# Attention stacks and the high halves of q and k: transposed by DMA instead of by TensorE and ScalarE, with SyncE in an order of steps of its own

## The reference, cut to what matters

```
x = x + cross_attention_16_heads(layernorm(x), ctx)       # stage n (projections) and stage a (attention)
x = x + quantised_ffn_with_conv(layernorm(x))              # stage b
x = x + cross_attention_1_head(layernorm(x), ctx)          # stage d
x = x + mixture_of_8_experts(layernorm(x))                 # stage c
```

```
q = rms_norm(x @ Wq + bq)                 # 16 heads of width 8
k, v = rms_norm(ctx @ Wk + bk), ctx @ Wv + bv
attn = softmax(q @ k.T / sqrt(8))         # per head, 128 x 120
out = (attn @ v) @ Wproj + bproj
```

## Time and profile before

| | us |
|---|---|
| median of 3 runs | 1326.22 (1324.22 to 1331.3) |
| the profiled execution, its own time | 1328.85 |
| its span, from the first to the last instruction | 1327.0 |
| TensorE busy | 1172.4 (88%) |
| VectorE busy | 1068.7 (81%) |
| ScalarE busy | 872.2 (66%) |
| GpSimd busy | 691.5 (52%) |
| chain of work that ended last | TensorE 60%, VectorE 29%, ScalarE 5% |

### The profile page before, as it was taken

How to read it: one execution, slowest core, us unless ns; L and a number is a source line. 1 busy time by engine, 2 the same in 40 slices (tenths; PEclk the granted TensorE clock), 3 DMA queues, 4 the chain that set the end, 5 groups by cost and what they waited for, 6 DMA issues and landing times.

```text
span 1327.0 us, 27899 instructions
## 1 busy us (share of the span) xinstructions
PE 1172.4 (88%) x10338; PEld 825.1 (62%) x10338; DVE 1068.7 (81%) x2837; ACT 872.2 (66%) x1684; POOL 691.5 (52%) x827
## 2 busy tenths in 40 slices
PE   1567578999999999999999999999999999989998
PEld 1334345776757676766767676767677576756665
DVE  4567786889899888889898998898888897767553
ACT  0245365868767676867777676768686676856554
POOL 3211214566564828374565738284756537365665
PEclk9567778999999999999999999999999899999999
DMA  6000001001010101010010101010100101000000
GB/s 190 20 13 9 20 16 28 17 15 38 3 42 9 43 9 36 16 37 16 5 41 10 43 9 43 9 36 17 35 17 6 31 1 36 16 9 16 9 8 9
DMA packets 63846, 32.69 MB, mean 25 GB/s; under 512 B 29280, under 2 KB 63072, under 8 KB 63328
## 3 DMA queue, kind: packets, MB, share of 16 engines
q1 hardware_dynamic: 61696, 26.83, 8.1%
q10 hardware_dynamic: 2016, 4.08, 0.8%
HBM read 24.73 MB, written 4.19 MB: 22 GB/s over the span
## 4 chain that ended last, share of the span: by engine, by line
PE 60%; DVE 29%; ACT 5%; issue 3%; POOL 1%; DMA 0%; SPq 0%; POOLq 0%; DVEq 0%; ACTq 0%
PE py L699 12%; PE pa L531 5%; DVE q_st L1075 4%; PE pg L682 3%; PE pa L495 3%; DVE moe L1196 3%; PE pa L519 3%; PE pu L682 3%; PE pg L684 3%; PE pg L683 3%; PE pu L683 3%; PE pu L684 3%; DVE acc L1209 2%; PE pb L579 2%; DVE stats L973 2%
## 5 line engine op out<-in xcount | busy, mean ns | idle before, releaser
L897 POOL TENSOR_TENSOR moe<-moe 128x512 f32<-128x512 f32 x256 | 325.0, 1272 | 410.0 <-DVE moe L1196 291.4
L699 PE MATMUL py<-wd_s,moe 128*128 128x128 f32 x2048 | 272.4, 277 | 1.7 <-ACT side L830 1.7
L699 PEld LDWEIGHTS py<-wd_s,moe 128*128 128x128 f32 x2048 | 258.0, 192 | 23.4 <-issue 3.8
L820 ACT ACTIVATE tg<-pg 128x512 f32<-128x512 f32 x256 | 153.2, 598 | 107.6 <-PE pg L684 106.0
L1075 DVE TENSOR_REDUCE q_st<-pa 128x4 f16<-128x480 f32 x256 | 167.7, 655 | 58.4 <-PE pa L495 58.3
L1196 DVE SCALAR_TENSOR_TENSOR moe<-tg,pg 128x512 f32<-128x512 f32 x256 | 174.0, 680 | 45.3 <-ACT tg L820 45.0
L834 ACT ACTIVATE moe<-pu 128x512 f32<-128x512 f32 x256 | 153.9, 601 | 33.4 <-PE pu L684 30.6
L758 ACT ACTIVATE probs<-pa 120x512 f32<-120x512 f32 x256 | 139.3, 602 | 16.7 <-PE pa L519 15.9
L495 PE MATMUL pa<-kbd,qkht 128*128 128x480 f16 x256 | 101.5, 397 | 38.6 <-DVE q_st L1075 33.4
L682 PE MATMUL pg<-x4h,wg_h 128*128 128x512 f16 x256 | 99.1, 387 | 14.9 <-DVE moe L1196 13.1
L682 PE MATMUL pu<-x4h,wu_h 128*128 128x512 f16 x256 | 99.0, 387 | 0.0
(11 more groups left out here) (182 smaller groups left out, 2529.0 us busy)
## 6 DMA issues: line engine op xcount, KB each, us to landing
xin<-in_x SPq DMA_DIRECT2D x16, 256.0 KB, 2.8
xres<-in_x SPq DMA_DIRECT2D x16, 256.0 KB, 3.0
kbd<-qkht SPq DMA_DIRECT2D x256, 7.5 KB
out_x<-acc SPq DMA_DIRECT2D x16, 256.0 KB, 4.1
ctxt_a<-in_ctx_t SPq DMA_DIRECT2D x16, 240.0 KB, 2.6
ctxt_b<-in_ctx_t SPq DMA_DIRECT2D x16, 240.0 KB, 3.5
ctxn_b<-in_ctx SPq DMA_DIRECT2D x16, 240.0 KB, 4.2
wd_s<-in_wd ACTq DMA_DIRECT2D x1, 1024.0 KB, 8.6
```

Of the source, the lines that this page charges most:

```text
L699: mm = pe.matmul(py[:, j, :], hu[:, u % 3, j * S:(j + 1) * S], wd_s[:, u, :], start=(half == 0 and j == 0), stop=(half == 1), skip_group_c ...
L820: act.activation(tg[:, u % 2, :], pg[:, :], ACT.Tanh, scale=0.5 / WSCALE).then_inc(tg_done.sem, 1)
L897: pool.tensor_tensor(hu[:, u % 3, :], gw[:, u % 3, :], us[:, u % 3, :], ALU.mult)\
```

## The change

What it does:

- Step `qkht` and step `stacks` no longer exist on TensorE and ScalarE. SyncE issues DMA transposes from SBUF to SBUF instead. For each group: one of `k_hi` (4 blocks of 128 x 128, fp16), one of `q_hi` (4 blocks), one of all k stacks of the group (16 blocks), and, for each t, one of the q stack (4 blocks). That is 7 DMAs and 40 blocks (1.31 MB) in each period.
- The q stack of t is double-buffered in `qs_t2`, the k stacks of a group in `ks_t2`. `k_st` is now single-buffered, and `kbd` is filled from `kht`.
- SyncE gets strings of its own in `TURNS`, and those of all other engines are written anew.
- `xq` and `p1n` are removed; their steps work in place in `xn2` and `p1`. Two waits come with that.

In the full period the steps of SyncE that do something stand in this order: `stacks` 0, `stacks` 1, load of xin, `stacks` 2, loads of ctxt_b and ctxn_b, load of ctxt_a, `stacks` 3, transpose of `k_hi` (in `rms_k`), transposes of `q_hi` and of the k stacks (in `rms_q`), the 16 DMAs into `kbd` (in `qkht`), store of the output, load of xres. On TensorE the new order between `max` (0, 3) and `scores` (0, 0) holds `g` 2, `u` 2, `d` 0, `g` 3 and `u` 3 of stage c; in `abdc` it holds `g` 2, `u` 2 and `d` 0. On VectorE the steps `fused` (one addition over 128 x 512) and `ln4` (a layernorm's statistics) now follow the making of `q_hi`; before they preceded it.

```
     "pe": {
...
-        "nabdc": ("bcadcacbaccacnacaccaaabaacadbcabccdbaaccabbaccbaacbabnadabcdbabccbacnaccabccnaacabacbccaadcabccd"
-                  "bacdacbacdnccccnabanacccdcbcacdbacca"),
...
+        "nabdc": ("accaacbcacccaccbanacaabcaaccbddccbcabdabcnbcanabcaabcbcancbaacanbdcbabcaaccacbccaaccdbaaccbadnad"
+                  "abccbaccdbcanccbaaccaccbaadcbadcacad"),
...
+    "sp": {
...
+        "nabdc": ("aacccccccbbbacacbabbcccacaacacaaaccacbnadccbaccdccbaacandabbccabcdcccccaaaadbaabdabdbbcacdbnccn"
+                  "dcbcadccabcaacaabbaaacnnbacccnacdaba"),
...
-        st_t = sb("st_t", [128, NQ * (S + SC)], F16)
+        qs_t2 = sb("qs_t2", [128, 2, NQ, S], F16)
+        ks_t2 = sb("ks_t2", [128, 2, GB, NQ, 128], F16)
...
+            def do_n(step, g):
+                if step == "xn1t" and g < NG - 1:
+                    sp.wait_ge(xn1_done.sem, xn1_done.at(g))
+                    sp.dma_start(xin[:, :, :], x_g[g + 1]).then_inc(xin_in.sem, 16)
+                elif step == "qkv" and g < NG - 1:
+                    sp.wait_ge(v_ps.sem, v_ps.at(g))
+                    sp.dma_start(ctxt_a[:, :, :], ctxt_g[g + 1]).then_inc(ctxa_in.sem, 16)
+                elif step == "rms_k":
+                    sp.wait_ge(kh_done.sem, kh_done.at(g))
+                    if later(g):
+                        for part in kbd_in:
+                            sp.wait_ge(part.sem, part.at(g - 1, 16 * HQ))
+                    sp.dma_start_transpose(kht[:, :, :], heads(k_hi)).then_inc(kht_in.sem, 16)
+                elif step == "rms_q":
+                    sp.wait_ge(q_hi_done.sem, q_hi_done.at(g))
+                    sp.dma_start_transpose(qht2[:, g % 2, :, :], heads(q_hi)).then_inc(qht_in.sem, 16)
+                    sp.wait_ge(dup_done.sem, dup_done.at(g, 2))
+                    sp.wait_ge(kl_done.sem, kl_done.at(g))
+                    if g >= 2:
+                        sp.wait_ge(s_ps.sem, s_ps.at(g - 2, 2 * GB))
+                    sp.dma_start_transpose(ks_t2[:, g % 2, :, :, :].rearrange("p t n s -> p (t n) s"),
+                                           k_st[:, :, :, :].rearrange("p t h d -> p (t h d)")).then_inc(ks_in.sem, 16)
+                elif step == "qkht":
+                    sp.wait_ge(kht_in.sem, kht_in.at(g, 16))
+                    if later(g):
+                        sp.wait_ge(max_ps.sem, max_ps.at(g - 1, 4 * GB))
...
+                        sp.dma_start(kbd[rows, :, h, :], kht[rows, :, 0:SC]).then_inc(kbd_in[h // HQ].sem, 16)
+
+            def do_a(step, g):
+                name, t, c = named(step)
+                if name == "stacks":
+                    if t == 0:
+                        sp.wait_ge(dup_done.sem, dup_done.at(g, 2))
+                        sp.wait_ge(ql_done.sem, ql_done.at(g))
+                    sp.wait_ge(max_done.sem, max_done.at(g, 4 * t + 4))
+                    if t >= 2:
+                        sp.wait_ge(s_ps.sem, s_ps.at(g, 2 * t - 2))
+                    elif later(g):
+                        sp.wait_ge(s_ps.sem, s_ps.at(g - 1, 2 * (GB + t) - 2))
+                    sp.dma_start_transpose(qs_t2[:, t % 2, :, :],
+                                           q_st2[:, g % 2, t, :, :].rearrange("p h d -> p (h d)")).then_inc(qs_in.sem, 16)
...
-                elif name == "stacks":
...
-                    take(BM, st_done, g, t + 1)
-                    for n in range(NQ):
-                        pe.transpose(pm16[:, n * S:(n + 1) * S], q_st[:, t, HQ * n:HQ * n + HQ, :], id_h[:, :])
-                    for n in range(NQ):
-                        mm = pe.transpose(pm16[:, NQ * S + n * SC:NQ * S + (n + 1) * SC],
-                                          k_st[0:SC, t, HQ * n:HQ * n + HQ, :], id_h[0:SC, 0:SC])
...
                     if c == 0:
-                        pe.wait_ge(st_done.sem, st_done.at(g, t + 1))
+                        if t == 0:
+                            pe.wait_ge(ks_in.sem, ks_in.at(g, 16))
+                        pe.wait_ge(qs_in.sem, qs_in.at(g, 16 * (t + 1)))
...
-                    act.activation(st_t[:, :], pm16[:, 0:NQ * (S + SC)], ACT.Copy).then_inc(st_done.sem, 1)
```

More of the change, by code:

```diff
@@ L80 @@
         "n": "nnnnnnn",
[L81 to L89, removed]
+        "wna": "nnaanaaaaaanaaanaawaaaaaaaaawaaawanaawwaaaaaaaaaaaaaan",
+        "nab": "aaabaaabababaaaanbbabaaaababbaanababaaaabbaaaanbabbaaababnnabaababbabnaan",
+        "nabd": "bbbbadaaabdnabbabbabaabadbanadabbaaaaanaabdaabaabdaabnaaaababnaaaddabanbaaadbnadbada",
+        "nabdc": ("abcaccacbcacccaacadacbaccacnbdcbccbbadancbbbcaaacacacbabaabccabdcccnacbcccaaabdcacaabdcabcbcnaca"
+                  "dcnbdaacnncaabccacbaccbcaacdadaccdab"),
+        "abdc": ("cabccacbacdcabaacccbaaccabadcabbcdabacdacccaabacbacaacacccabbcabaacccabcacbccdacaaccdccbadbccaba"
+                 "aabacaadcdbccacbdcbccabdcacba"),
+        "bdc": "cbccbcccdcbcbbbccbdcbcdbbcccbbcbcccdcbccccccddbccbccbcccdccbbddcccbcccbcdcccbccbdbc",
+        "dc": "cccccccccccccccddccccdccccdcdcccccccdccddccdccccccccccccddc",
         "c": "cccccccccccccccccccccccccccccccccccccccccccccccc",
@@ L106 @@
         "n": "nnnnnnn",
[L107 to L113, removed]
@@ new lines, in do_d, with do_c @@
+            def do_d(step, g):
+                if step == "oc" and g < NG - 1:
+                    sp.wait_ge(oc_ps.sem, oc_ps.at(g))
+                    sp.dma_start(ctxt_b[:, :, :], ctxt_g[g + 1]).then_inc(ctxb_in.sem, 16)
+                    sp.dma_start(ctxn_b[0:SC, :, :], ctx_g[g + 1]).then_inc(ctxb_in.sem, 16)
+            def do_c(part, g):
+                if part == ("d", NU - 1):
+                    sp.wait_ge(sum_done.sem, sum_done.at(g, len(SIDE)))
+                    sp.dma_start(out_g[g], acc2[:, :, :]).then_inc(out_done.sem, 16)
@@ L426, in _, with idle @@
+            def idle(step, g):
+                pass
+            periods(sp, lambda n, a, b, d, c: run_turns("sp", n, a, b, d, c, idle, do_n, do_a, idle, do_d, do_c))
             sp.wait_ge(out_done.sem, out_done.at(NG - 1, 16))
@@ L473, in do_n @@
                     mm.then_inc(v_ps.sem, 1)
-                elif step == "qkht":
-                    qkh = bank("qkht").bitcast(F16)
-                    pe.wait_ge(q_hi_done.sem, q_hi_done.at(g))
-                    take(BANK["qkht"], qkht_done, g)
-                    for j in range(GB):
-                        pe.transpose(qkh[:, j * S:(j + 1) * S], q_hi[:, j, :], id_h[:, :])
-                    pe.wait_ge(kh_done.sem, kh_done.at(g))
-                    for j in range(GB):
-                        mm = pe.transpose(qkh[:, GB * S + j * SC:GB * S + (j + 1) * SC], k_hi[0:SC, j, :],
-                                          id_h[0:SC, 0:SC])
-                    mm.then_inc(qkht_ps.sem, 1)
             def do_a(step, g):
                 name, t, c = named(step)
-                q_st, k_st, v_st = q_st2[:, g % 2, :, :, :], k_st2[:, g % 2, :, :, :], v_st2[:, g % 2, :, :, :]
+                v_st, ks_t, qs_t = v_st2[:, g % 2, :, :, :], ks_t2[:, g % 2, t, :, :], qs_t2[:, t % 2, :, :]
                 if name == "max":
@@ L634, in do_d @@
                     for j in range(GB):
-                        mm = pe.transpose(pd[0:SC, j * S:(j + 1) * S], p1n[:, j, :], id_f[:, :])
+                        mm = pe.transpose(pd[0:SC, j * S:(j + 1) * S], p1[:, j, :], id_f[:, :])
                     mm.then_inc(p1t_ps.sem, 1)
```

162 lines of the change are left out of this document (74 added, 88 removed).

## The result

The changed kernel takes 1351.12 us (median of 4 runs, 1349.64 to 1353.46); the kernel before, measured beside it, 1327.83. The ratio is 1.0177, with a 95% interval of 1.0144 to 1.0211. The forecast was 1315, on the other side of no change; 1351 lies in its range. The span of the profiled execution is 1349.5 us against 1327.0, 22.5 us more.

A forecast was written before the change was run, and what follows sets the result against it. It took TensorE to bound full periods, VectorE close behind. Removed work -31.8, stalls +11.7 and early periods +8.9 summed to -11.2 us, hence 1315 us; range 1298 to 1395, likeliest case 1301 to 1326.

The forecast's parts named there:

- The step that failed: Full periods: TensorE busy 69 of 72 us, VectorE 65 and 7 behind, so work taken off TensorE counts.
- Rival 2: VectorE sets the full period, so relief and stall vanish and +8.9 us of early periods remain: 1335 us; chance 0.12.
- Removed work: TensorE's transposes and its wait for the first stack's copy: 2.51 us per full period, 31.8 us in all.
- The price of a transpose: SyncE's time issuing a DMA transpose: 1.04 us for a q stack, 2.1 us for the k stacks.
- The stall at the first stack: TensorE before scores (0, 0): latency 3.2 us, 2.4 covered, 0.8 open; 2.1 in abdc; together 11.7 us.
- SyncE's queue and kbd: Full periods: kbd's last quarter arrives 1.2 us before it is needed; k stacks may cost SyncE 3.3 us.
- Rival 1: SyncE's queue late with kbd behind the k stacks: 1369 to 1465 us; chance 0.20 at moderate prices, 0.12 near upper bound.
- Early periods: wna, nab, nabd: q stack latency 7.2 us, plus 1.7 for the first kbd being late; 8.9 us added.
- The clock (rival 3): New stall lowers the granted clock in every second full period, adding 39 us: 1354 us; chance 0.06.

The follow-up runs named there:

- the long memsets: GpSimd's 256 multiplies gw * us replaced by three memsets each, product left out: changed kernel 1301.98 us, kernel before 1321.90 us.
- the halves: Each GpSimd multiply gw * us done as two of 256 columns, nothing left out: changed kernel 1320.82 us, kernel before 1343.86 us.
- the run with each twice: Changed kernel with a second DMA transpose of 4 blocks, into a spare tile, behind each of the seven from the third group on: 1363.47 us.
- the old order: Changed kernel with TensorE, ScalarE, VectorE and GpSimd in the kernel before's order of steps, SyncE keeping its new one: 1422.46 us.

## Why the prediction was wrong

**The step that failed** is in the first paragraph of the forecast and in its sum: that VectorE "gets nothing off" and "is 7 us behind" in a full period, taken as a fixed 65 us, so that TensorE's relief counts in full. The 7 us are the distance to the period's 72; to TensorE's 69 it was 3.7 us, not much more than the 2.5 us that the change was to take from TensorE. In the changed kernel VectorE is busy 68.0 us in such a period (747.66 / 11) against 65.9 (724.36 / 11), because the new order sets more of its instructions beside GpSimd's reading ones. With the GpSimd reads of the multiply gone, the same kernel has 63.5 (635.07 us in the ten periods from 288.01 to 998.29). Rival 2 named the right engine (12%) and priced it at 1335: it took VectorE's own time as unchanged, and was 16 us short.

The sum, set against the pairs (medians): without the multiply's reads the change is worth 1301.98 - 1321.90 = -19.9 us. Those reads cost 49.1 us in the changed kernel and 5.4 in the kernel before, 43.7 more. -19.9 + 43.7 = 23.8 us is the change as measured; the four times are only arranged anew here, so this proves nothing by itself, but it gives the sizes. With the multiply's reads out of the way there was a gain, larger than the forecast of -11, and with them it was more than given back. That the 43.7 us are meetings, and not GpSimd's busy time, rests on the long memsets and on the halves.

**Removed work: right in kind, somewhat too large.** Forecast 2.51 us for each full period, 27.6 for eleven. In the pair with the long memsets eleven periods took 780.8 us (288.01 to 1068.85) against 801.0 (289.58 to 1090.55): 20.1 less, 1.8 a period, with no stall against it. TensorE is busy 19.9 us less there, but VectorE 13.7 less too, so the 1.8 us can't all be put down to TensorE with certainty.

**The price of a transpose: right.** 1.19 to 1.26 and 1.87 us, forecast 1.04 and 2.1, from bounds a factor of eight and thirty apart. Of the two pages of the Trainium skill that the forecast weighs, "VectorE: DVE Perf Modes", section "The three transpose paths", would have a block cost 1309 ns; as time of the queue that is not borne out: 16 blocks hold it for 1.87 us, 12 blocks more cost about 0.65 us more, some 0.055 each.

**The stall at the first stack: wrong by its size, harmless.** Forecast a latency of 3.2 us and 0.8 of it open. The landing takes 2.4 us from the start of the issue, not 2.2 after its end (836.69 + 2.2 would be 838.89, after the scores had begun at 838.54), so the latency is 835.33 to 837.87, 2.5 us; the lower end of what was given (2.6) was the right one. The scores came 3.2 us after the reduction (838.54 - 835.33), 0.3 of them a wait of TensorE for VectorE in stage c, so the cover was some 2.9 us and not 2.4, and nothing is left open. In abdc no wait for qs_t appears either. The sum had 11.7 us too many. (The lower end of the forecast's range is also off by a little: with a q stack at 2.6 us the stalls come to 12 x 0.2 + 1.5 = 3.9, which is 7.8 us less, not 9.)

**SyncE's queue and kbd: right.** kbd is in time in every full period; moving it ahead changes nothing (1350.25). Rival 1's mechanism is real: it sets in once four more transposes stand right ahead of kbd (the run with each twice), but not here; it is what makes the old order 71 us worse, by the wait for GpSimd's copies and not by the price of an issue.

**Early periods: 8.0 us, forecast 8.9**, which looks right. But in the pair with long memsets the fifth row differs by -1.6 (288.01 against 289.58), and the kernel before has it anywhere from 284.36 to 289.58 in the variants with the same order. So the agreement may be chance; what the early periods cost by the new latency wasn't settled. All of TensorE's waits for qs_t lie there, 12.7 us before matmuls. And the clock differs there, which the forecast's 8.9 us left out; the changed kernel first, then the kernel before, in the columns of the earlier trace rows:

```profile
0.00:292.34 292.34, 187.53 (x1492) 119.03 (x1492) 202.48 (x515) 118.92 (x218) 85.19 (x119) 0.74 0.24 56
```

```profile
0.00:284.36 284.36, 190.41 (x1681) 126.69 (x1682) 200.22 (x517) 138.43 (x238) 83.98 (x122) 0.80 0.13 37
```

The granted clock is 0.74 against 0.80, with TensorE busy less. How much of the 8.0 us that is, no run shows.

**The clock (rival 3): not where it was forecast.** It is 0.99 in the eleven periods of both. Ahead of them it is lower in the changed kernel, as just said; the early periods, clock and all, are 8.0 us of the 22.5.

**What stays open:** whether an order exists in which the DMA transposes are covered and VectorE's instructions of two inputs stay clear of GpSimd's; with the present one, and three memsets in place of the multiply, the measured time is 1302, but then the product is missing. Splitting the other reading instructions of GpSimd (the copies L883 and L888, the additions L917) was not tried.

## What to carry to other kernels

Before an order of steps is changed, look at which VectorE instructions with two SBUF inputs (residual additions, gated products, scalings by a tile) fall beside a GpSimd instruction that reads SBUF: compare the mean with the shortest of each form, because the wait stands in the profile as busy time and under no semaphore. Look at small `tensor_scalar` instructions too: beside a multiply, an addition or a memset of GpSimd they ended with it. An engine at 81% can be the one whose time counts; test it by taking work from it, not by its share. And where a long GpSimd instruction can't be moved, cut it in two: 30 us here, but measure it, since in the kernel before the same cut cost 16.

## What the runs showed that was not expected

- A VectorE instruction of 128x512 with two SBUF inputs started beside a reading GpSimd instruction ends 0.54 to 0.55 us after that one's end, up to 1.2 us later than alone (1.87 against 0.69); GpSimd's waits the same way (1.18 against 0.73).
- A `tensor_scalar` of 4 elements a lane is caught too, with a factor from SBUF (1.30 us instead of 0.22) or with constants alone (0.74 instead of 0.17), and also by a memset (0.38 instead of 0.17). It ends 0.01 to 0.04 us behind GpSimd's instruction.
- SBUF to SBUF transposes hold SyncE's queue for 1.19 to 1.26 us (4 blocks) and 1.87 us (16), and land 2.4 and 4.3 us after the issue begins; 16 plain DMAs over 8 partitions each hold it for 11.7 to 12.4.
